# Flags of the block candidates: one comparison of all blocks on VectorE, their sum over blocks on TensorE, over tiles on ScalarE

## The chip, the cores and the metric
The kernel runs on one core of one Trainium2 chip. The metric is the device time of one execution in microseconds (us). Of the kernel before, 3 runs are given; a profile was taken in one more execution, and all durations below come from that one.

## The reference
The input is 16 batches of 512 tokens with 256 features. One transformer layer is computed, in float32: attention with 16 heads of width 16, residual and layer norm, then a gated feed-forward part (256 to 768 to 256), residual and layer norm. The attention is sparse: of the 512 scores of a row only those not below the row's 31st largest are kept.

```python
def proj(W, b):
    return (x @ W.T + b).reshape(B, L, H, D).transpose(0, 2, 1, 3)
scores = jnp.einsum('bhqd,bhkd->bhqk', Q, K) / math.sqrt(D)
top_vals, _ = jax.lax.top_k(scores, U)          # U = 31
thresh = top_vals[..., -1:]
scores = jnp.where(scores < thresh, -jnp.inf, scores)
attn = jax.nn.softmax(scores, axis=-1)
context = jnp.einsum('bhqk,bhkd->bhqd', attn, V)
...
x = _layernorm(x + attention(x))
x = _layernorm(x + (silu(x @ wg.T) * (x @ wu.T)) @ wd.T)
```

## The kernel before, in words
**Tiles and slots.** A tile is 128 query rows of one head against all 512 keys, so a batch has 16 heads x 4 = 64 tiles (`TILES`), and the kernel 1024. Every engine runs the same loop of 64 slots per batch, written out, and in slot n it works on several tiles at once, each at its own stage: the lags at the top of the file (`COUNT0 = 1`, `COUNT1 = 2`, `BELOW = 4`, ... `PV = 25`, `GROUP = 41`) say how many slots after its scores a tile comes to each stage. Semaphores tie the engines together; the order on each engine is fixed by `slots`.

**How a threshold is found.** TensorE makes a tile's scores (L593), VectorE copies them out with a shift and notes the row's maximum (`evacuate`, L859). ScalarE counts twice with Sign how many scores of a row lie above a guessed threshold (`count_first` L459, `count_second` L468); both have an accumulator output. TensorE writes the scores that lie below the guess once more into `Y_ps` (L603, L604, L606). Of each of the 4 blocks of 128 columns (`BLOCKS`) VectorE takes the 8 largest into `cand` (L866), and then the 16 largest of these 32 into `best` (L879, L882, L886). The count tells which of the 16 is the 31st of the row. That choice is made for 8 tiles (two heads) at a time, which the code calls a pair (`PAIR = 8`); there are 8 pairs in a batch and 128 in the kernel.

**The steps of a pair, on VectorE.** `pick` in slots with n % 8 = 6 marks the ranks that are not wanted (L897, 128 x 128 elements) and reduces `hidden`, the largest over the 4 blocks of each block's 8th candidate (L900). `pick_candidate` in the next slot combines the marks with `best` (L907). `pick_threshold` in slots with n % 8 = 0 reduces the chosen value (`least`, L915), compares `hidden` with it (`flag`, L917: 8 flags and, by the accumulator output, their sum as a ninth column), and adds the shift (`thr`, L921). A flag of 1 says that a block may hold more than 8 of the wanted values, so that the threshold can't be trusted.

**The way of a flag.** In the same slot TensorE adds the flags over the 128 rows, one float32 matmul against a column of ones into a PSUM bank called `bench` (`sum_flags`, L646 to L649, at the end of its slot). In the next slot ScalarE copies the 9 numbers as integers to `flag_i` (`copy_flags`, L448), behind the exponential of that slot and ahead of both counts. VectorE loads the ninth into a register after the slot's evacuation (`check`, L945); if it is above zero it loads the 8 others (L948) and finds the threshold of each flagged tile anew with four MAX8 over the whole row (`general`, L923 to L938). Then it releases the pair's thresholds to GpSimd (`thr_done`, L953), which makes the masks of its 8 tiles (`cut`, L1080, L1082 and 8 times L1088). TensorE adds the masks to the transposed scores (L617, L620), ScalarE takes the exponential (L476), TensorE multiplies by V (L634). The two `bench` banks are handed round by the semaphores `ready` and `taken`, and a flag's use of a bank is one of those of `uses_of`.

**Other work** is spread over the slots by tables: projections (L547, L578), transposes, output projection (L663), the feed-forward part (L670, L676), residuals and layer norms.

Of the kernel before, what the change touches and what calls it, by code (L numbers as in the profile page):

```python
# [12 lines left out]
P = 128  # L13
# [13 lines left out]
GONE = -3.0e38  # L27
# [13 lines left out]
BLOCKS = 4  # L41
# [21 lines left out]
RING = 32  # L63
S_PLACES = 22
MASKS = 4
CANDS = 16
PAIR = 2 * NT
# [17 lines left out]
F32 = mybir.dt.float32  # L85
F32R = mybir.dt.float32r
I32 = mybir.dt.int32
BF16 = mybir.dt.bfloat16
ALU = mybir.AluOpType
ACT = mybir.ActivationFunctionType  # L90
AX = mybir.AxisListType
# [68 lines left out]
def tile_place(part):  # L160
    return part % 2, part // 2


def build(nc, xT, x, wqT, wkT, wvT, woT, bq, bk, bv, bo, wgT, wuT, wdT, ident_in, blocks_in, heads_in, ranks_in, out):
    with ExitStack() as ctx:
        def sb(name, shape, dt=F32):
            return ctx.enter_context(nc.sbuf_tensor(name, shape, dt))

        def ps(name, shape):
            return ctx.enter_context(nc.psum_tensor(name, shape, F32))  # L170

        def sem(name):
            return ctx.enter_context(nc.semaphore(name))
# [7 lines left out]
        heads_r = sb("heads_r", [P, HALF], F32R)  # L181
        ranks = sb("ranks", [P, RANKS])
        ones = sb("ones", [1, P])
        onesc = sb("onesc", [P, 1])
        wqk = [sb(f"w{n}", [P, C, DM]) for n in "qk"]
        bqk = [sb(f"b{n}", [P, 2]) for n in "qk"]
        wv = sb("wv", [P, C, DM])
# [59 lines left out]
        cand = sb("cand", [P, CANDS, BLOCKS, 8])  # L247
# [2 lines left out]
        other = sb("other", [P, PAIR, RANKS])  # L250
        picked = sb("picked", [P, PAIR, RANKS])
        least = sb("least", [P, PAIR])
        hidden = sb("hidden", [P, PAIR])
        flag = sb("flag", [P, 2, PAIR + 1])
        flag_i = sb("flag_i", [1, 2, 16], I32)
        W = sb("W", [P, L])
        gtop = sb("gtop", [P, 4, 8])
# [7 lines left out]
        bench = [ps(f"bench{i}", [P, L]) for i in range(2)]  # L265
# [10 lines left out]
        taken = [sem(f"taken{i}") for i in range(2)]  # L276
# [14 lines left out]
        flag_done = sem("flag_done")  # L291
# [28 lines left out]
        def of_pair(a, g):  # L320

            h = 2 * g % HALF
            return a[:, 2 * g // HALF, :].rearrange("p (t h) -> p h t", h=HALF)[:, h:h + 2, :]

        def by_head(a):
            return a.rearrange("p (h t) -> p h t", h=2)
# [72 lines left out]
        def _(act):  # L399
# [42 lines left out]
            def copy_flags(b, n, first, at):  # L442
                k, use = at
                g = (n - CHECK) // PAIR
                act.wait_ge(ready[k], use + 1)
                if not (first and n < CHECK + 2 * PAIR):
                    act.wait_ge(thr_done, b * NP + g - 1)
                nc.scalar.activation(flag_i[0:1, g % 2, 0:PAIR + 1], bench[k][0:1, 0:PAIR + 1], ACT.Copy).then_inc(taken[k], 1)  # L448

            def count_first(T, n, b, first):  # L450
                j = (n - COUNT0) % TILES
# [92 lines left out]
        def _(pe):  # L544
            def project(what, hb, k):
                for c in range(C):
                    mm = nc.tensor.matmul(bench[k][:, :], wqk[what][:, c, hb * P:(hb + 1) * P], xTs[:, c, :],  # L547
                                          start=(c == 0), stop=(c == C - 1))
                return mm

            def keys(k):
                for t in range(NT):
                    mm = nc.tensor.matmul(bench[k][:, t * P:(t + 1) * P], hi[1][:, t * P:(t + 1) * P], ident_r[:, :],
                                          start=True, stop=True)
                return mm

            def gram_matrix(k):
                for t in range(NT):
                    mm = nc.tensor.matmul(bench[k][:, 0:P], Kn[:, t, :], Kn[:, t, :], start=(t == 0), stop=(t == NT - 1))
                return mm  # L560

            def quadratic(k):
                return nc.tensor.matmul(bench[k][:, :], gram[:, :], hi[0][:, :], start=True, stop=True)
# [82 lines left out]
            def sum_flags(b, n, k):  # L646
                g = (n - THRESHOLD) // PAIR
                pe.wait_ge(flag_done, b * NP + g + 1)
                return nc.tensor.matmul(bench[k][0:1, 0:PAIR + 1], onesc[:, :], flag[:, g % 2, :], start=True, stop=True)  # L649

            def turn_rows(src, k):

# [100 lines left out]
            for i, what in enumerate(PROLOGUE):  # L753
                k, use = tile_place(i)
                if use:
                    pe.wait_ge(taken[k], use)
                if what in ("q", "k"):
                    mm = project("qk".index(what), 0, k)
                if what == "keys":
                    pe.wait_ge(hi_done, 2)  # L760
                    mm = keys(k)
                if what == "gram":
                    pe.wait_ge(taken[0], 2)
                    mm = gram_matrix(k)
                if what == "quad":
                    pe.wait_ge(taken[1], 2)
                    mm = quadratic(k)
                if what == "sums":
                    pe.wait_ge(taken[0], 3)
                    mm = row_sums(k)  # L770
# [4 lines left out]
            for c in range(C):  # L775
                nc.tensor.matmul(bench[0][0:1, 0:DM], bvc[:, c:c + 1], wo[:, c, :], start=(c == 0), stop=False)
            nc.tensor.matmul(bench[0][0:1, 0:DM], ones[:, 0:1], brow[:, :],
                             start=False, stop=True).then_inc(brow_done, 1)
# [8 lines left out]
        def _(dve):  # L787
            steps = [0]

            def mark(ins):  # L790
                ins.then_inc(dve_step, 1)
                steps[0] += 1
                return steps[0]
# [94 lines left out]
            picks = {}  # L888

            def pick(b, n):  # L890

                g = (n - PICK) // PAIR
                r, e = g * PAIR % RING, g * PAIR % CANDS
                dve.wait_ge(cnt1_done, b * TILES + (g + 1) * PAIR)
                if sorted_to[0]:
                    dve.wait_ge(dve_step, sorted_to[0])
                picks["other"] = mark(nc.vector.tensor_tensor(  # L897
                    other[:, :, :], ranks[:, :].unsqueeze(1).to_broadcast([P, PAIR, RANKS]),
                    s1[:, r:r + PAIR].unsqueeze(2).to_broadcast([P, PAIR, RANKS]), ALU.not_equal))
                picks["hidden"] = mark(nc.vector.tensor_reduce(hidden[:, :], cand[:, e:e + PAIR, :, 7], AX.X, ALU.max))  # L900

            def pick_candidate(n):
                g = (n - PICKED) // PAIR
# [5 lines left out]

            def pick_threshold(n):  # L910
                g = (n - THRESHOLD) // PAIR % NP
                r, c = g * PAIR % RING, g % 2
                if "picked" in picks:
                    dve.wait_ge(dve_step, picks["picked"])
                t = mark(nc.vector.tensor_reduce(least[:, :], picked[:, :, :], AX.X, ALU.max))  # L915
                dve.wait_ge(dve_step, t)
                nc.vector.scalar_tensor_tensor(out=flag[:, c, 0:PAIR], in0=hidden[:, :], scalar=GONE, in1=least[:, :],  # L917
                                               op0=ALU.max, op1=ALU.is_gt,
                                               accum_out=flag[:, c, PAIR:PAIR + 1]).then_inc(flag_done, 1)

                picks["kept"] = mark(nc.vector.tensor_tensor(by_head(thr[:, r:r + PAIR]), by_head(least[:, :]), of_pair(na, g), ALU.add))  # L921

# [17 lines left out]
            def check(n, at):  # L940
                k, use = at
                g = (n - CHECK) // PAIR
                c = g % 2
                wait_apart(dve, taken[k], use + 1)
                some = dve.value_load(flag_i[0:1, c, PAIR:PAIR + 1], min_val=0, max_val=PAIR * P)  # L945
                with dve.If(some > 0):
                    for t in range(PAIR):
                        flagged = dve.value_load(flag_i[0:1, c, t:t + 1], min_val=0, max_val=P)  # L948
                        with dve.If(flagged > 0):
                            general((g * PAIR + t) % TILES)  # L950
                if "kept" in picks:
                    dve.wait_ge(dve_step, picks["kept"])
                dve.nop(nofuse=True).then_inc(thr_done, 1)  # L953
# [225 lines left out]
```

## Time and profile before

| | |
|---|---|
| median of 3 runs | 3387.09 us |
| lowest, highest | 3374.43, 3392.51 us |
| the profiled execution, its own time | 3384.81 us |
| its span | 3383.0 us |
| mean granted TensorE clock | 0.913 of full speed |
| busy share: TensorE / VectorE / ScalarE / GpSimd | 83% / 76% / 71% / 71% |

The span runs from the first to the last instruction; 1.8 us of the execution lie outside it. PE is TensorE's matmuls, PEld its weight loads, DVE VectorE, ACT ScalarE, POOL GpSimd, and a trailing q an engine's sequencer, which handles waits, registers and branches. An instruction with an accumulator output shows as two, the second of which is named READ_ACCUMULATOR.

### The profile page before, as it was taken

To read this page: it belongs to the slowest core of one execution; us is meant where nothing else is said; L and a number is where in the kernel's file an instruction comes from. 1 tells how busy PE (TensorE), PEld (TensorE's weight loads), DVE (VectorE), ACT (ScalarE), POOL (GpSimd) and SP (SyncE) were. 2 spreads that over 40 slices of the span, in tenths; PEclk is the share of its full clock that TensorE was granted. 3 is DMA by queue.
4 is the path that set the end of the run, shared out by engine and by line. 5 is a ranking of instruction groups with operands and counts; after the bars stand their busy time and mean duration, and the time that the engine had idled before them with its cause. 6 is when DMAs were issued, how large, how long until landed. Compare 5 with 4: busy or idle time off the path is not lost.

```text
span 3383.0 us, 82396 instructions
## 1 busy us (share of the span) xinstructions
PE 2808.2 (83%) x21094; PEld 1534.9 (45%) x21439; DVE 2587.7 (76%) x12511; ACT 2414.3 (71%) x5894; POOL 2405.8 (71%) x1677
## 2 busy tenths in 40 slices
PE   5889899697989888776998999987789976886986
PEld 2344545344444444433544454544445443443454
DVE  4888788787878787777887888887778877777861
ACT  4788787686868787665786788886668865675862
POOL 2787788586777786656786787876668865675881
PEclk7799999899999898987998999998889988898986
DMA  3101011110101111011110111111011110111000
GB/s 82 43 23 43 22 41 31 33 26 19 44 24 35 25 35 35 18 32 23 27 42 21 36 24 46 27 37 32 17 33 27 46 25 15 33 26 27 20 14 7
DMA packets 91071, 102.84 MB, mean 30 GB/s; under 512 B 34417, under 2 KB 52850, under 8 KB 90482
## 3 DMA queue, kind: packets, MB, share of 16 engines
q1 hardware_dynamic: 88448, 93.73, 11.6%
q8 instruction: 186, 3.05, 0.4%
q14 instruction: 403, 3.30, 0.3%
q10 hardware_dynamic: 2034, 2.76, 0.2%
HBM read 20.86 MB, written 8.39 MB: 9 GB/s over the span
## 4 chain that ended last, share of the span: by engine, by line
PE 44%; DVE 19%; issue 15%; ACT 11%; POOL 4%; DVEq 4%; SPq 1%; ACTq 0%; DMA 0%; POOLq 0%
DVE cand L866 6%; PE Y_ps L606 5%; PE bench L676 5%; PE ST_ps L620 5%; PE ST_ps L617 5%; PE ctxT_ps L634 5%; PE bench L670 4%; ACT junk L459 4%; PE Y_ps L604 3%; POOL mask L1088 3%; ACT above L468 3%; DVEq L948 3%; PE bench L547 2%; ACT PT L476 2%; DVE S L859 2%
## 5 line engine op out<-in xcount | busy, mean ns | idle before, releaser
L1088 POOL TENSOR_SCALAR mask<-S,thr,mb 128x512 bf16<-128x512 f32 x1024 | 2117.6, 2084 | 43.0 <-POOL mb L1082 24.8
L866 DVE MAX8 cand<-Y_ps 128x8 f32<-128x128 f32 x4096 | 1069.2, 281 | 9.9 <-issue 9.8
L459 ACT ACTIVATE junk<-S,nt 128x512 bf16<-128x512 f32 x1024 | 733.7, 716 | 476.4 <-DVE S L859 472.9
L859 DVE TENSOR_SCALAR_CACHE_REDUCE S<-S_ps,na 128x512 f32<-128x512 f32 x1024 | 755.6, 738 | 298.8 <-PE S_ps L593 246.4
L468 ACT ACTIVATE above<-S,s,steep 128x512 bf16<-128x512 f32 x1024 | 822.5, 803 | 0.0
L476 ACT ACTIVATE PT<-ST_ps 128x512 f32<-128x512 f32 x1024 | 596.6, 583 | 199.0 <-PE ST_ps L620 196.6
L1080 POOL TENSOR_SCALAR rbig<-rmax 128x8 f32<-128x8 f32 x128 | 31.3, 244 | 755.2 <-DVEq L953 755.1
L617 PE MATMUL ST_ps<-QS,KS 64*128 64x512 f32 x1024 | 463.4, 453 | 94.3 <-ACT PT L476 89.7
L593 PE MATMUL S_ps<-KS,QS 64*128 64x512 f32 x1024 | 532.3, 520 | 4.2 <-DVE S L859 2.2
L606 PE MATMUL Y_ps<-KS,QS 64*128 64x512 f32 x1024 | 532.1, 520 | 1.0 <-issue 0.7
L604 PE MATMUL Y_ps<-above,nbig 128*128 128x512 bf16 x1020 | 406.6, 399 | 146.8 <-DVE cand L866 107.6
L603 PE MATMUL Y_ps<-ones_b,nbig 128*128 128x512 bf16 x683 | 276.6, 405 | 268.7 <-DVE cand L866 259.7
L620 PE MATMUL ST_ps<-nbig,mask 128*128 128x128 bf16 x4096 | 424.3, 229 | 0.0
L606 PEld LDWEIGHTS Y_ps<-KS,QS 64*128 64x128 f32 x1024 | 195.1, 190 | 469.0 <-issue 469.0
L620 PEld LDWEIGHTS ST_ps<-nbig,mask 128*128 128x128 bf16 x4096 | 241.4, 100 | 339.7 <-issue 339.7
L634 PE MATMUL ctxT_ps<-PT,V 128*32 128x128 f32 x8192 | 346.6, 289 | 0.0
L603 PEld LDWEIGHTS Y_ps<-ones_b,nbig 128*128 128x128 bf16 x1024 | 101.4, 99 | 502.2 <-issue 450.4
L879 DVE MAX8 best<-cand 128x8 f32<-128x32 f32 x1024 | 191.9, 187 | 142.9 <-issue 140.9
L617 PEld LDWEIGHTS ST_ps<-QS,KS 64*128 64x128 f32 x1024 | 199.9, 195 | 203.2 <-ACT PT L476 195.4
L634 PEld LDWEIGHTS ctxT_ps<-PT,V 128*32 128x32 f32 x8192 | 201.2, 113 | 57.9 <-issue 7.2
L593 PEld LDWEIGHTS S_ps<-KS,QS 64*128 64x128 f32 x1024 | 195.3, 191 | 5.3 <-DVE S L859 3.3
L459 ACT ACTIVATION_READ_ACCUMULATOR junk<-S,nt 128x1 f32 x1024 | 196.3, 192 | 0.0
(121 smaller groups left out, 3837.7 us busy)
## 6 DMA issues: line engine op xcount, KB each, us to landing
QS<-Qhi SPq DMA_DIRECT2D x512, 32.0 KB, 2.0
KS<-Khi SPq DMA_DIRECT2D x512, 32.0 KB, 2.0
KS<-Klo SPq DMA_DIRECT2D x512, 32.0 KB, 2.0
QS<-Qlo SPq DMA_DIRECT2D x512, 32.0 KB, 2.0
xTs<-in_xT SPq DMA_DIRECT2D x17, 512.0 KB, 3.8
xs<-in_x SPq DMA_DIRECT2D x16, 512.0 KB, 3.9
out<-xs SPq DMA_DIRECT2D x16, 512.0 KB, 2.9
hT<-in_wgT ACTq DMA_DIRECT2D x1, 768.0 KB
```

The costliest lines, as they stand in the source:

```text
L459: nc.scalar.activation(junk[:, :], S[:, score_place(j)[0], :], ACT.Sign, bias=nt0[:, hb, col:col + 1], scale=-1.0, accum_out=s0[:, j % 8:j ...
L468: nc.scalar.activation(above[:, j % 4, :], S[:, score_place(j)[0], :], ACT.Sign, bias=s0[:, j % 8:j % 8 + 1], scale=steep[:, hb, col:col + ...
L476: nc.scalar.activation(PT[:, j % 4, :], ST_ps[:, :], ACT.Exp, scale=SCALE).then_inc(exp_done, 1)
L593: nc.tensor.matmul(S_ps[n % 2][:, :], QS[rows, r, q:q + P], KS[rows, r, :], start=True, stop=True, tile_position=(rows.start, 0)).then_inc ...
L604: nc.tensor.matmul(Y[:, :], nbig[:, :], above[:, j % 4, :], start=False, stop=False)
L606: nc.tensor.matmul(Y[:, :], QS[rows, r, q:q + P], KS[rows, r, :], start=False, stop=True, tile_position=(rows.start, 0)).then_inc(below_do ...
L617: nc.tensor.matmul(ST_ps[:, :], KS[rows, r, kt * P:(kt + 1) * P], QS[rows, r, :], start=True, stop=False, tile_position=(rows.start, 0))
L620: mm = nc.tensor.matmul(ST_ps[:, t * P:(t + 1) * P], mask[:, h % MASKS, t, kt * P:(kt + 1) * P], nbig[:, :], start=False, stop=(t == NT - 1))
L634: mm = nc.tensor.matmul(ctxT_ps[32 * a:32 * a + 32, strip * P:(strip + 1) * P], V[:, k, grp, strip * VW:strip * VW + 32], PT[:, (j - kt + ...
L859: nc.vector.tensor_scalar(S[:, at, :], S_ps[n % 2][:, :], na[:, hb, col:col + 1], None, ALU.add, op1=ALU.max, accum_out=rmax[:, n % RING:n ...
L866: mx = nc.vector.max(cand[:, j % CANDS, i, :], Y_ps[j % 2][:, i * BW:(i + 1) * BW])
L1088: nc.gpsimd.tensor_scalar(mask[:, h % MASKS, t, :], S[:, score_place(j)[0], :], thr[:, r:r + 1], mb[:, r:r + 1], ALU.is_lt, op1=ALU.add).t ...
```

## The change
VectorE no longer reduces `hidden`. Instead it compares all 4 blocks' 8th candidates with `least` in one tensor_tensor, whose 128 x 32 flags are written as bfloat16. TensorE adds the blocks by 4 accumulating bfloat16 matmuls of 8 columns (one per block, each reading every fourth flag). ScalarE's copy now covers 8 columns and makes their sum by its accumulator output, in float32; VectorE reads its bits as an integer, which is above zero where the sum is.

```diff
-        onesc = sb("onesc", [P, 1])
+        onesc = sb("onesc", [P, 1], BF16)
...
-        hidden = sb("hidden", [P, PAIR])
-        flag = sb("flag", [P, 2, PAIR + 1])
+        flag = sb("flag", [P, 2, PAIR, BLOCKS], BF16)
...
-                nc.scalar.activation(flag_i[0:1, g % 2, 0:PAIR + 1], bench[k][0:1, 0:PAIR + 1], ACT.Copy).then_inc(taken[k], 1)
+                nc.scalar.activation(flag_i[0:1, g % 2, 0:PAIR], bench[k][0:1, 0:PAIR], ACT.Copy,
+                                     accum_out=flag_i[0:1, g % 2, PAIR:PAIR + 1].bitcast(F32)).then_inc(taken[k], 1)
...
-                return nc.tensor.matmul(bench[k][0:1, 0:PAIR + 1], onesc[:, :], flag[:, g % 2, :], start=True, stop=True)
+                for i in range(BLOCKS):
+                    mm = nc.tensor.matmul(bench[k][0:1, 0:PAIR], onesc[:, :], flag[:, g % 2, :, i], start=(i == 0),
+                                          stop=(i == BLOCKS - 1))
+                return mm
...
-                picks["hidden"] = mark(nc.vector.tensor_reduce(hidden[:, :], cand[:, e:e + PAIR, :, 7], AX.X, ALU.max))
...
-                nc.vector.scalar_tensor_tensor(out=flag[:, c, 0:PAIR], in0=hidden[:, :], scalar=GONE, in1=least[:, :],
-                                               op0=ALU.max, op1=ALU.is_gt,
-                                               accum_out=flag[:, c, PAIR:PAIR + 1]).then_inc(flag_done, 1)
+                nc.vector.tensor_tensor(flag[:, c, :, :], cand[:, e:e + PAIR, :, 7],
+                                        least[:, :].unsqueeze(2).to_broadcast([P, PAIR, BLOCKS]),
+                                        ALU.is_gt).then_inc(flag_done, 1)
...
-                some = dve.value_load(flag_i[0:1, c, PAIR:PAIR + 1], min_val=0, max_val=PAIR * P)
+                some = dve.value_load(flag_i[0:1, c, PAIR:PAIR + 1], min_val=0, max_val=0x45000000)
...
-                        flagged = dve.value_load(flag_i[0:1, c, t:t + 1], min_val=0, max_val=P)
+                        flagged = dve.value_load(flag_i[0:1, c, t:t + 1], min_val=0, max_val=BLOCKS * P)
```

## Rows read from the trace of the kernel before

**Rows 1.** The page: busy time by engine, the chain that ended last.
```profile
PE 2808.2 (83%) x21094; PEld 1534.9 (45%) x21439; DVE 2587.7 (76%) x12511; ACT 2414.3 (71%) x5894; POOL 2405.8 (71%) x1677
...
PE 44%; DVE 19%; issue 15%; ACT 11%; POOL 4%; DVEq 4%; SPq 1%; ACTq 0%; DMA 0%; POOLq 0%
```

**Rows 2.** The chain in order of time, 1055.9 to 1060 us: start, us, what.
```profile
1056.16 0.42 PE Y_ps L606
...
1056.65 0.76 DVE S L859 x2
1057.41 0.21 DVE least L915
...
1058.15 0.08 DVE flag L917
...
1059.82 0.38 PE Y_ps L604
```

**Rows 3.** Timeline of VectorE around a pick: start, us, engine, line, operation, shapes.
```profile
1033.05 0.20 DVE L900 TENSOR_REDUCE hidden<-cand 128x8 f32<-128x32 f32 x1
1033.17 0.18 DVE L879 MAX8 best<-cand 128x8 f32<-128x32 f32 x1
```

**Rows 4.** The chain's pieces at L900: the first and the last of 33.
```profile
70.72 0.12 DVE hidden L900
...
3107.41 0.13 DVE hidden L900
```

**Rows 5.** Single lines of VectorE: duration in ns, minimum/median/maximum.
```profile
L897 DVE TENSOR_TENSOR other<-ranks,s x128: 278/286/1554, 70.4 to 3272.9; 128x128 f32<-128x128 f32 x128
...
L917 DVE SCALAR_TENSOR_TENSOR flag<-hidden,least x128: 166/170/1402, 75.1 to 3274.4; 128x8 f32<-128x8 f32 x128
...
L921 DVE TENSOR_TENSOR thr<-least,na x128: 159/166/1380, 75.2 to 3274.5; 128x8 f32<-128x8 f32 x128
```

**Rows 6.** Groups of VectorE by line: busy us, mean ns of one, idle before.
```profile
L917 DVE SCALAR_TENSOR_TENSOR flag<-hidden,least 128x8 f32<-128x8 f32 x128 | 45.3, 354 | 4.4
...
L900 DVE TENSOR_REDUCE hidden<-cand 128x8 f32<-128x32 f32 x128 | 26.2, 205 | 0.0
...
L917 DVE DVE_READ_ACCUMULATOR flag<-hidden,least 128x1 f32 x128 | 10.2, 80 | 0.0
```

**Rows 7.** Timeline around a stretched comparison: VectorE, then GpSimd.
```profile
1143.86 0.67 DVE L917 SCALAR_TENSOR_TENSOR flag<-hidden,least 128x8 f32<-128x8 f32 x1
...
1144.46 0.08 DVE L917 DVE_READ_ACCUMULATOR flag<-hidden,least 128x1 f32 x1
1144.46 0.16 DVE L921 TENSOR_TENSOR thr<-least,na 128x8 f32<-128x8 f32 x1
...
1143.75 2.07 POOL L1088 TENSOR_SCALAR mask<-S,thr,mb 128x512 bf16<-128x512 f32 x1
```

**Rows 8.** Timeline of TensorE around the sum of flags; then its matmuls alone.
```profile
1146.48 0.14 PEld L649 LDWEIGHTS bench<-flag,onesc 128*1 128x1 f32 x2
...
1146.54 0.20 PE L649 MATMUL bench<-flag,onesc 128*1 128x9 f32 x2
...
L649 PE MATMUL bench<-flag,onesc x256: 170/173/222, 76.6 to 3281.4; 128*1 128x9 f32 x128
```

**Rows 9.** The chain at matmuls of 8 columns with 128 columns of weights.
```profile
1169.65 0.11 PE bench L569
```

**Rows 10.** The chain's pieces at L649: the first and the last of 37.
```profile
96.95 0.13 PE bench L649 x2
...
3238.26 0.03 PE bench L649
```

**Rows 11.** Timeline of ScalarE around the copy of flags.
```profile
1147.22 0.15 ACT L448 ACTIVATE flag_i<-bench 1x9 int32<-1x9 f32 x1
...
1147.28 0.71 ACT L459 ACTIVATE junk<-S,nt 128x512 bf16<-128x512 f32 x1
...
1147.89 0.18 ACT L459 ACTIVATION_READ_ACCUMULATOR junk<-S,nt 128x1 f32 x1
...
1147.99 0.80 ACT L468 ACTIVATE above<-S,s,steep 128x512 bf16<-128x512 f32 x1
```

**Rows 12.** The chain's pieces at L448: the first and the last of 13.
```profile
340.75 0.15 ACT flag_i L448
...
3216.31 0.02 ACT flag_i L448
```

**Rows 13.** A check that waits for its flags: the copy, the load, VectorE's next work.
```profile
L448 ACT ACTIVATE flag_i<-bench x1: 153/153/153, 1220.9 to 1220.9; 1x9 int32<-1x9 f32 x1
...
L945 DVEq TENSOR_LOAD <-flag_i x1: 307/307/307, 1221.3 to 1221.3; - x1
...
1222.61 0.20 DVE L879 MAX8 best<-cand 128x8 f32<-128x32 f32 x1 [0.68 <-issue]
```

**Rows 14.** A check that doesn't: the same three.
```profile
L448 ACT ACTIVATE flag_i<-bench x1: 153/153/153, 1060.3 to 1060.3; 1x9 int32<-1x9 f32 x1
...
L945 DVEq TENSOR_LOAD <-flag_i x1: 304/304/304, 1061.0 to 1061.0; - x1
...
1062.35 0.19 DVE L879 MAX8 best<-cand 128x8 f32<-128x32 f32 x1 [0.43 <-issue]
```

**Rows 15.** The chain in an opened pair, and the count of tile loads.
```profile
1121.34 0.30 DVEq L948
...
1122.16 0.31 DVEq L948
...
L948 DVEq TENSOR_LOAD <-flag_i x184: 298/303/910, 119.6 to 3127.4; - x184
```

**Rows 16.** Waits, the longest in total: us, times, longest.
```profile
POOL rbig L1080 <- DVEq L953: 755.1, 107, 37.0
```

More of the change, by code:

```diff
@@ L892, in pick @@
                 g = (n - PICK) // PAIR
-                r, e = g * PAIR % RING, g * PAIR % CANDS
+                r = g * PAIR % RING
                 dve.wait_ge(cnt1_done, b * TILES + (g + 1) * PAIR)
@@ L911, in pick_threshold @@
                 g = (n - THRESHOLD) // PAIR % NP
-                r, c = g * PAIR % RING, g % 2
+                r, c, e = g * PAIR % RING, g % 2, g * PAIR % CANDS
                 if "picked" in picks:
```

## The prediction
> **What bounds the kernel now.** I read the shares of the engines first, then the chain of work that ended last. No engine is full: TensorE 83% busy, VectorE 76%, ScalarE and GpSimd 71% [rows 1]. The chain stands on TensorE for 44%, on VectorE for 19%, on ScalarE for 11%, on GpSimd for 4% [rows 1], and changes engine within a few microseconds: at 1056 us it leaves TensorE for VectorE's evacuation, passes through the very instructions of the change, and is back on TensorE at 1059.8 [rows 2]. So no engine's busy time can be used as a price. The change takes a little from VectorE and puts a little on TensorE and ScalarE, once in each of 128 pairs. I therefore price each edit by the time that its engine is held until it starts the next instruction, and multiply by the pairs in which the chain stands on that engine there. All sums start from the profiled execution, 3384.81 us, 2.3 us below the median of the runs.
>
> **The reduction of `hidden` goes.** It lasts 205 ns [rows 6], but the next MAX8 starts 0.12 us after it [rows 3], and the chain gives it 0.12 us too [rows 4]. The chain holds it in 33 of 128 pairs [rows 4]: 33 x 0.12 = -4.0 us. Elsewhere VectorE reaches its next wait earlier; that is worth nothing while TensorE or ScalarE sets the pace. Bounds: 0, and 128 x 0.12 = -15.4 us if VectorE paced every pair.
>
> **The comparison changes form.** The row before is a comparison of 8 elements, median 170 ns. The new one has 32 elements and no accumulator. A tensor_tensor of 8 elements takes 166 ns, one of 128 elements 286 ns [rows 5], 1.0 ns an element, so 32 make about 190 ns: 0.02 us more. The accumulator's read of 80 ns [rows 6] starts in the same instant as the next instruction at 1144.46 [rows 7], so I credit nothing for it. I find the chain on VectorE at the comparison in 48 pairs: 48 x 0.02 = +1.0 us. The bounds are -0.08 us a pair, if the read does hold the engine, and +0.02 us.
>
> The mean of the old comparison is 354 ns against the median of 170 [rows 5, 6]: 128 x 0.184 = 23.6 us of stretch. In the row shown it lasts 0.67 us, while GpSimd's mask has started 0.11 us before [rows 7]. Both the old and the new form read two tensors of SBUF, so the stretch should stay, and I cost it at 0. If it went, 48 of 128 pairs' share would be -8.9 us; if timing moved more comparisons into a mask's start, as much could be added.
>
> **TensorE.** Before, one float32 matmul runs as two weight loads and two passes; both together last 0.20 us, one alone 0.17 [rows 8], so a further pass costs 0.03 us. The change makes four weight loads and four bfloat16 passes: two more, +0.06 us. The bound above is the 0.11 us of a pass of 8 columns that loads 128 weight columns [rows 9], +0.22 us; below, nothing. I take 0.06, since its row has one weight column as the new ones have. The chain holds L649 in 37 pairs [rows 10], and stands on TensorE there in 41: 41 x 0.06 = +2.5 us (0 to 9; over all pairs 7.7).
>
> The Trainium skill, "TensorE: Matmul & The Clock Gate", section "Back-to-back issue gap", speaks against this: streams of weight load and matmul are spaced by about 81 ns at 128 columns, whereas an isolated matmul of 1 to 64 columns has a floor near 25 ns. By the first, two more would cost 0.16 us, as an estimate, and this term would be 6.6 us; the row of two passes 0.03 us apart is on the side of the second.
>
> **ScalarE.** The copy holds the engine for 0.06 us (1147.22 to 1147.28). An accumulator output adds a read; behind that of the first count the next instruction starts 0.10 us after the read [rows 11], 0.09 us in most places. So +0.09 us a pair: the exponential of the slot is ahead of it, both counts behind it and with them TensorE's L604 and the next exponential. The chain stands on ScalarE at the copy in 21 pairs, in 13 of which it holds the copy itself [rows 12]: 21 x 0.09 = +1.9 us (bounds 0 and 128 x 0.09 = 11.5).
>
> **The flag comes later to the check.** The copy signals after 0.15 us now; with the read it is 0.06 + 0.19 = 0.25 us [rows 11], and where ScalarE waited for TensorE, 0.06 more: 0.15 us late. Queued behind the check on VectorE are the sort of the next tile and its evacuation; GpSimd waits for it 755 us in all [rows 16]. A load that waits for the copy starts some 0.17 us after the copy's end. There are 9 such pairs among 128, the one at 1220.9 shown; VectorE then sits idle for 0.68 us [rows 13] instead of 0.43 [rows 14]. All others have more time: the next 24 loads start 0.34 to 0.42 us after the copy's end, 0.17 us or more to spare. So 9 x 0.15 = +1.4 us.
>
> **What stays.** The flagged tiles are the same: the largest of four values exceeds `least` exactly when one of them does. 184 tile loads are 23 opened pairs [rows 15], after as before. DMAs and the other uses of the banks are untouched.
>
> **The sum.** -4.0 + 1.0 + 2.5 + 1.9 + 1.4 = +2.8 us; 3384.8 + 2.8 = 3387.6, and I give 3388. A measurement of this kernel can tell about 0.5% from no change, 17 us.
>
> **Rival 1, VectorE paces more than the chain shows: faster.** Then each pair gives back its 0.12 us (-15.4), the comparison is no longer held by GpSimd on the chain (-8.9), and ScalarE's +1.9 remains: 3384.8 - 22.4 = 3362. For it: the chain's 15% of issue time, much of it VectorE's sequencer. Against it: the wait of ScalarE and GpSimd is mostly for other things than these instructions, and the new form has two SBUF inputs as well. The Trainium skill, "SBUF — State Buffer", section "SBUF: two separate sides", says that a VectorE operation with two SBUF inputs and a GpSimd operation exclude each other for a whole instruction; the trace shows the exclusion, but its comparison ended 0.78 us into a mask of 2.07 us. By that rule too the new form is held as the old. Chance 0.12.
>
> **Rival 2, the late flag becomes a new wait: slower.** Place: the load of the check. If the flag is late by d, 9 pairs pay d, 24 pay d less about 0.2, and 20 more, whose load starts 0.42 to 0.6 us after the copy, pay d less about 0.34. At d = 0.6 us, from four weight loads that wait for one another and an accumulator that drains slowly, this is 5.4 + 9.6 + 5.2 = 20 us, and 3405 in all. It decides from d of about 0.55 us; I expect 0.15. Chance 0.10.
>
> **Rival 3, the change doesn't do what it says: slower.** If the bits of the float sum, or the integer conversion, opened pairs without a flag, each would cost 8 loads 0.8 us apart [rows 15], 6.4 us; 105 unflagged pairs make at most 670 us, and 20 already 128: 3513. The sum of zeros has zero bits, so I give 0.02.
>
> **How the numbers follow.** My case has 0.76. Its own range: the gains at their bound and the losses at none give 3384.8 - 15.4 = 3369; TensorE's at 9, ScalarE's at 11.5 and the check's 1.4 with no gain give 3407. The runs shown themselves spread over 18 us. Leaving the corners out, 3371 to 3406 should hold 8 in 10; Rival 1's point and Rival 3 lie outside, Rival 2's just inside. Faster by over 0.5%: Rival 1's 0.12, of which some falls short of 17 us, and scatter of the runs in my case: 0.12. Slower: Rivals 2 and 3 with scatter, 0.13. Within: 0.75.
>
> **What would show it.** In the changed profile: no L900 group, VectorE busy down by some 26 + 10 us less 3 for the longer comparison; the comparison's median near 190 ns with maxima above 1 us still; TensorE's group of the flags with 512 short passes, first to last within 0.3 us; a READ_ACCUMULATOR of 0.19 us behind the copy, ScalarE busy up by some 25 us; 184 tile loads. Wrong would be: a chain that gives the check or the flags' matmuls 20 us more, a comparison never above 0.2 us, more than 184 tile loads, or another granted clock than 0.91.

## The result, and the profile after

The changed kernel takes 3410.53 us (median of 8 runs, 3401.91 to 3418.27), the kernel before 3385.31 us beside it (8 runs, 3374.43 to 3398.04): a ratio of 1.0078, with a 95% interval of 1.006 to 1.0095. That is 25 us slower, 22 us above the forecast of 3388 and above the upper end of its range, 3406.

The page of the changed kernel, busy time by engine, the chain's shares and the queue of instruction transfers:

```profile
span 3406.6 us, 83125 instructions
...
PE 2885.9 (85%) x21695; PEld 1551.2 (46%) x21695; DVE 2579.7 (76%) x12255; ACT 2429.4 (71%) x6022; POOL 2404.5 (71%) x1677
...
q14 instruction: 400, 3.28, 0.3%
...
PE 45%; DVE 20%; issue 15%; ACT 11%; DVEq 4%; POOL 3%; SPq 1%; ACTq 0%; DMA 0%; POOLq 0%
```

Beside [rows 1] this hardly shows a change. VectorE has 8 us less work, ScalarE 15 us more; the records of TensorE can't be compared this closely, since [rows 1] hold 21094 matmuls beside 21439 weight loads, where each matmul has one. No engine took over the chain.

The groups that the change touches, by line (busy us, mean ns of one, idle before):

```profile
L921 DVE TENSOR_TENSOR flag<-cand,least 128x32 bf16<-128x32 f32 x128 | 48.7, 380 | 4.4
...
L448 ACT ACTIVATION_READ_ACCUMULATOR flag_i<-bench 1x1 f32 x128 | 23.8, 186 | 0.0
...
L448 ACT ACTIVATE flag_i<-bench 1x8 int32<-1x8 f32 x128 | 19.8, 155 | 3.2 <-PE bench L651 1.1
```

And the same as single lines, with minimum, median and maximum in ns:

```profile
L651 PE MATMUL bench<-flag,onesc x512: 167/168/214, 76.2 to 3306.7; 128*1 128x8 bf16 x171
...
L921 DVE TENSOR_TENSOR flag<-cand,least x128: 207/219/1424, 74.7 to 3298.9; 128x32 bf16<-128x32 f32 x128
...
L952 DVEq TENSOR_LOAD <-flag_i x184: 296/303/890, 120.0 to 3146.4; - x184
```

The reader is to see that every instruction of the change is of the kind and nearly of the length that was forecast, and that there are still 184 tile loads, 23 opened pairs [rows 15]. A pair's flags in the timeline of 1060 to 1075 us, for the four passes and the late sum:

```profile
1068.26 0.24 PEld L651 LDWEIGHTS bench<-flag,onesc 128*1 128x1 bf16 x4
1068.37 0.25 PE L651 MATMUL bench<-flag,onesc 128*1 128x8 bf16 x4
...
1069.59 0.15 ACT L448 ACTIVATE flag_i<-bench 1x8 int32<-1x8 f32 x1
1069.65 0.19 ACT L448 ACTIVATION_READ_ACCUMULATOR flag_i<-bench 1x1 f32 x1
```

Where the time went shows only in the waits. Waits of the changed kernel (idle us, times, the longest one):

```profile
POOL rbig L1084 <- DVEq L957: 776.6, 113, 35.9
...
DVE best L883 <- issue: 159.6, 112, 6.4
```

Of the kernel before, the same view has for the second line:

```profile
DVE best L879 <- issue: 140.9, 114, 6.4
```

GpSimd waits 21.5 us longer for the release of the pairs' thresholds (755.1 [rows 16]; L957 is the release that was L953), and VectorE stands 18.7 us longer before the sort L883 that follows the check, for "issue", which is nothing that the profile shows. The release is a step that the change doesn't touch.

### The profile page after: what moved, and what is told of

The parts are those of the page before. It is cut to its first block, busy times and chain, and to the rows that moved or that the text cites. A ratio compares the mean times of both kernels' runs of the same rounds, so it can differ in the third digit from the quotient of the medians.

```text
span 3406.6 us, 83125 instructions
## 1 busy us (share of the span) xinstructions
PE 2885.9 (85%) x21695; PEld 1551.2 (46%) x21695; DVE 2579.7 (76%) x12255; ACT 2429.4 (71%) x6022; POOL 2404.5 (71%) x1677
## 3 DMA queue, kind: packets, MB, share of 16 engines
q14 instruction: 400, 3.28, 0.3%
## 4 chain that ended last, share of the span: by engine, by line
PE 45%; DVE 20%; issue 15%; ACT 11%; DVEq 4%; POOL 3%; SPq 1%; ACTq 0%; DMA 0%; POOLq 0%
DVE cand L870 7%; PE Y_ps L607 5%; PE bench L680 5%; PE bench L674 5%; PE ST_ps L618 5%; PE ST_ps L621 5%; PE ctxT_ps L635 4%; ACT junk L460 4%; PE Y_ps L604 3%; PE Y_ps L605 3%; PE bench L548 3%; DVEq L952 3%; ACT above L469 3%; DVE S L863 3%; POOL mask L1092 2%
## 5 line engine op out<-in xcount | busy, mean ns | idle before, releaser
L870 DVE MAX8 cand<-Y_ps 128x8 f32<-128x128 f32 x4096 | 1081.1, 286 | 7.3 <-issue 7.0
L604 PE MATMUL Y_ps<-ones_b,nbig 128*128 128x512 bf16 x1024 | 414.0, 404 | 364.9 <-DVE cand L870 351.3
L883 DVE MAX8 best<-cand 128x8 f32<-128x32 f32 x1024 | 195.0, 190 | 161.6 <-issue 159.6
```

The lines of the kernel that those rows point to most:

```text
L604: nc.tensor.matmul(Y[:, :], nbig[:, :], ones_b[:, :], start=True, stop=False)
L870: mx = nc.vector.max(cand[:, j % CANDS, i, :], Y_ps[j % 2][:, i * BW:(i + 1) * BW])
```

## The parts by themselves

The first four kernels ran on one chip. `a_full` is the changed kernel again, and the reference for the three others.

> The whole change again, on the chip of the three below, so that the parts are compared with it and with the kernel before on one chip. Every theory: 3410 us, ratio 1.0078 or so, granted clock near 0.906.

Measured: 3402.7 us, ratio 1.0039 (1.0022 to 1.0056), span 3407.5 us. The same code was timed twice more (below), with 1.0077 and 1.0078. So four timings of one kernel gave 1.0039 to 1.0078, and differences of 0.4% between two kernels of this study are to be read with care.

**TensorE alone**: the flags and the column of ones in bfloat16, and the same nine columns added four times.

```diff
-                return nc.tensor.matmul(bench[k][0:1, 0:PAIR + 1], onesc[:, :], flag[:, g % 2, :], start=True, stop=True)
+                for i in range(BLOCKS):
+                    mm = nc.tensor.matmul(bench[k][0:1, 0:PAIR + 1], onesc[:, :], flag[:, g % 2, :],
+                                          start=(i == 0), stop=(i == BLOCKS - 1))
+                return mm
```

> TensorE's part alone: the flags and the ones are bfloat16, and the same nine columns are added four times. Theory 1 (the parts add up by their occupancy): four passes cost 0.06 us more in 41 pairs, +2.5 us, 3388. Theory 2 (TensorE's part carries the change, since the flags' passes stand on TensorE's own path): +15 to 20 us, 3402. Theory 3 (small shifts move the clock's dips and code fetches): anywhere between 3380 and 3405, with the granted clock going along.

Measured: 3379.66 us, 0.9983 (0.9968 to 0.9998), span 3382.5. Two more passes a pair cost nothing that is seen.

**ScalarE alone**: the copy of 8 columns with the accumulator output, everything else as before.

> ScalarE's part alone: 8 columns are copied and their sum is made by the accumulator output. Theory 1: +0.09 us in 21 pairs and a check later by 0.10 us in 9, +3 us, 3388. Theory 4 (ScalarE holds the path longer than the chain showed, up to all 128 pairs): +0.1 x 128 = +13 us, 3398. If it is above 3398, the late flag of Rival 2 is in play and the idle of VectorE behind the check grows.

Measured: 3386.46 us, 0.9999 (0.9986 to 1.0013), span 3385.7. The read is there, at 185 ns, and the flag comes as late to the check as in the change. It costs nothing:

```profile
L448 ACT ACTIVATION_READ_ACCUMULATOR flag_i<-bench 1x1 f32 x128 | 23.7, 185 | 0.0
```

**The change without ScalarE's part**: VectorE writes the sum itself, as a ninth row, and ScalarE copies 9 columns.

```diff
-                nc.vector.tensor_tensor(flag[:, c, :, :], cand[:, e:e + PAIR, :, 7],
-                                        least[:, :].unsqueeze(2).to_broadcast([P, PAIR, BLOCKS]),
-                                        ALU.is_gt).then_inc(flag_done, 1)
+                nc.vector.scalar_tensor_tensor(out=flag[:, c, 0:PAIR, :], in0=cand[:, e:e + PAIR, :, 7], scalar=GONE,
+                                               in1=least[:, :].unsqueeze(2).to_broadcast([P, PAIR, BLOCKS]),
+                                               op0=ALU.max, op1=ALU.is_gt,
+                                               accum_out=flag[:, c, PAIR, 0:1]).then_inc(flag_done, 1)
```

> The change with ScalarE's part undone: the comparison of 32 elements sums its own flags by an accumulator output, TensorE adds four passes of nine columns, ScalarE copies nine. Theory 1: 3410 less 3 = 3407. Theory 4: 3410 less 13 = 3397. Theory 2 (TensorE's part carries the change): 3408. If VectorE's new comparison is what costs, 3408 or above.

Measured: 3396.8 us, 1.0034 (1.0021 to 1.0048), span 3393.9. So the loss comes with VectorE's part: the parts that leave VectorE's instructions alone lose nothing, and the two kernels in which a pair has fewer of them lose. Their own durations don't explain it: the new comparison is 0.05 us longer (219 ns against 170), which makes 6 us in all 128 pairs, and what was taken out should gain, not lose.

## A check that stalls

The page doesn't show what differs at the check, single instances do. The same check (batch 5, slot 25) is quick in the kernel before: load at 1061.0 [rows 14], and the release 1.2 us later:

```profile
L953 DVEq EVENT_SEMAPHORE  x1: 21/21/21, 1062.2 to 1062.2; - x1
```

In `a_full` (line, duration, first to last start; the second line is the release):

```profile
L949 DVEq TENSOR_LOAD <-flag_i x1: 305/305/305, 1067.6 to 1067.6; - x1
...
L957 DVEq EVENT_SEMAPHORE  x1: 21/21/21, 1071.2 to 1071.2; - x1
```

VectorE's timeline around it, and GpSimd's:

```profile
1067.80 0.73 DVE L863 TENSOR_SCALAR_CACHE_REDUCE S<-S_ps,na 128x512 f32<-128x512 f32 x1
1068.46 0.08 DVE L863 DVE_READ_ACCUMULATOR S<-S_ps,na 128x1 f32 x1
1071.38 0.20 DVE L883 MAX8 best<-cand 128x8 f32<-128x32 f32 x1 [2.83 <-issue]
...
1065.49 2.07 POOL L1092 TENSOR_SCALAR mask<-S,thr,mb 128x512 bf16<-128x512 f32 x1
1071.35 0.24 POOL L1084 TENSOR_SCALAR rbig<-rmax 128x8 f32<-128x8 f32 x1 [3.79 <-DVEq L957]
```

The release comes 3.55 us after the load, VectorE is idle for 2.83 us instead of 0.43 [rows 14], and GpSimd with it. The flag was zero: no tile load lies between. VectorE's sequencer only had to branch over the block that finds flagged tiles anew. The kernel before has the same stall in other places, such as batch 2, slot 9, which is quick in `a_full` (1.18 us):

```profile
L945 DVEq TENSOR_LOAD <-flag_i x1: 303/303/303, 416.3 to 416.3; - x1
...
L953 DVEq EVENT_SEMAPHORE  x1: 21/21/21, 420.0 to 420.0; - x1
```

```profile
416.87 0.08 DVE L859 DVE_READ_ACCUMULATOR S<-S_ps,na 128x1 f32 x1
420.16 0.20 DVE L879 MAX8 best<-cand 128x8 f32<-128x32 f32 x1 [3.21 <-issue]
```

Of the 128 checks, 105 open no pair in every kernel. From load to release they take 1.18 us (median); a few take 2.2 to 3.8. Taken over all 105, from the trace of each:

| | sum, us | over 1.5 us |
|---|---|---|
| before | 148.2 | 12 |
| TensorE alone, ScalarE alone | 147.9, 147.5 | 12, 12 |
| changed kernel, and `a_full` | 155.0, 155.2 | 16, 16 |
| change without ScalarE's part | 161.1 | 21 |

The stalls belong to places in the code, not to moments: VectorE's loop holds five batches written out, and a stalled check stalls again five batches later (in `a_full` slot 25 of batches 5, 10 and 15, slot 57 of batches 3, 8 and 13). Before, TensorE alone and ScalarE alone have one and the same set. The change takes two instructions a pair out of VectorE's code, L900 and the accumulator's read behind L917, so that each later check sits at another place.

Counted in instructions along VectorE's stream (the skipped block is 136 of them), the checks of the kernel before, of `a_full` and of the change without ScalarE's part that take over 2.1 us are those at which the jump lands on number 62 to 78 of a run of 128. Every closed check that lands on 62 to 77 stalls; of two places that land on 78 one does; none that lands elsewhere takes more than 1.7 us. The count can be off by one or two. 128 instructions are, if the 8192 bytes of one instruction transfer (400 transfers with 3.28 MB on the page above) are theirs, 64 bytes each. The trace's records of these transfers agree: after a quick check's load one of 8192 bytes starts at about 1.78 us, 0.6 us behind the release; after that of 763.26 us in `a_full` one starts at 1.64 us, a second at 4.17, and the release, at 3.56, lies behind the first. This holds beyond the two. In the kernel before, each of the 12 stalled checks has one transfer of 8192 bytes that starts between its load and its release, and the release comes 1.76 to 2.01 us behind that start; in the 93 other closed checks none starts there. (In `a_full` 3 of 89 quick checks have one as well, 0.2 to 0.4 us behind the load.) That is how I read it: the engine waits for code.

The Trainium skill, "Runtime: NRT & Kernel Launch", section "Instruction fetch mechanics", says that code is fetched ahead in sequence and that a "taken branch whose target isn't in the current 2-page window forces a DMA fetch of the target page before execution can continue". The traces agree with that, and show its price here, 1.1 to 2.5 us a branch. That section of the Trainium skill gives blocks of 16 KiB or 256 instructions; here VectorE's stalls repeat with 128, and the transfers beside them have 8192 bytes.

## Moving the code and nothing else

If place is the cause, a kernel with other places and the same work must show it. The first try put instructions of the sequencer alone, `dve.nop(nofuse=True)`, ahead of VectorE's loop.

> The whole change, with 26 empty instructions ahead of VectorE's first wait for loads, so that all its later code lies 26 instructions further on and nothing else differs. In the traces so far a closed check (one that opens no pair) takes 1.18 us from its load to its release, or 2.2 to 3.7 us, and the slow ones come back every 5 batches, which is the unrolling of VectorE's loop. Theory L (the place of the branch's target in VectorE's code decides: slow where it falls on instruction 62 to 78 of every 128, counted from the trace's first): slow closed checks cost 6 us instead of 28 to 31, 3402.7 - 22 = 3380, granted clock up to 0.915. Theory T (it is timing, not place): 3403, with the same 16 slow checks.

> The whole change, with 39 empty instructions at the same place. Theory L: 23 checks' places are slow, 48 us in all, 20 more than unshifted: 3403 + 20 = 3423. Theory T: 3403.

> The kernel before, with 111 empty instructions at the same place. Theory L: slow checks cost 5 us instead of 25, 3387 - 20 = 3367. Theory T: 3387. Against the change shifted by 26, which has about the same cost of slow checks, it gives the change without its effect on the code's place: under the predicted sum of parts 3 us apart; if more than 10 us apart, the new comparison or the way of the flags costs by itself.

> The kernel before, with 78 empty instructions at the same place. Theory L: slow checks cost 41 us instead of 25, 3387 + 16 = 3403, as slow as the change. Theory T: 3387.

Measured: 1.0077 (1.0057 to 1.0096), 1.0078 (1.0059 to 1.0098), 0.9999 (0.9984 to 1.0013), 0.9998 (0.9984 to 1.0013). The stalled checks are the same ones as without the instructions, 16 and 12 of them: a nop that signals nothing left nothing in the code, and these four are repeats of the two kernels. What they say is how well a repeat agrees: within 0.1% on one chip.

The second try used memsets of one column of a tensor that nothing reads, once, ahead of VectorE's first wait:

```diff
+        filler = sb("filler", [P, P])
...
+            for _ in range(78):
+                nc.vector.memset(filler[:, _:_ + 1], 1.0)
```

> As b_full26, but with 26 real instructions: memsets of one column of an unused tensor ahead of VectorE's first wait for loads, where it idles for 11 us. (The trace of b_full26 shows that the empty instructions had not been kept: VectorE's code began as before and the same 16 closed checks were slow, so those four runs were repeats of the change and of the kernel before.) Theory L (place in VectorE's code): slow closed checks at 6 us over the usual 1.18 each instead of 31: 3410 - 25 = 3385 or, where TensorE's clock gains too, 3378. Theory T (timing, not place): 3410, 16 slow checks.

> The change with 39 such memsets. Theory L: some 23 slow closed checks, 48 us in all, 17 to 20 more than unshifted: 3410 + 18 = 3428. Theory T: 3410.

> The kernel before with 111 such memsets. Theory L: slow checks 5 us in all instead of 25: 3385 - 20 = 3365. Theory T: 3385. The change shifted by 26 against this one is the change without the code's place.

> The kernel before with 78 such memsets. Theory L: slow checks 41 us in all instead of 25: 3385 + 16 = 3401. Theory T: 3385.

| | ratio | interval | sum of the 105 checks, us | over 1.5 us |
|---|---|---|---|---|
| change + 26 | 1.0053 | 1.0035 to 1.0071 | 132.9 | 8 |
| change + 39 | 1.0072 | 1.0056 to 1.0089 | 175.5 | 26 |
| before + 111 | 0.9982 | 0.9971 to 0.9993 | 145.3 | 15 |
| before + 78 | 1.0111 | 1.0091 to 1.0132 | 170.0 | 25 |

The last row shows that place alone can cost this much. It is the kernel before, without any part of the change, its code 78 instructions further on, and it takes 3422.05 us, 37 us more than the kernel before on the same chip (3385.08) and more than the change. Its span, and the waits of GpSimd for the release:

```profile
die 0 (median of its cores): 3423.2 us, clock 0.908
```

```profile
POOL rbig L1083 <- DVEq L954: 795.0, 112, 35.5
```

40 us of wait more than in [rows 16], 21.8 us of it in the closed checks themselves. One of them, batch 5, slot 57, takes 1.16 us before and 3.63 here:

```profile
1189.23 0.08 DVE L860 DVE_READ_ACCUMULATOR S<-S_ps,na 128x1 f32 x1
1192.53 0.19 DVE L880 MAX8 best<-cand 128x8 f32<-128x32 f32 x1 [3.22 <-issue]
```

The unused tensor and the memsets themselves are not the cause: before + 111 has the same tensor and more memsets, and is 0.2% faster than the kernel before.

Only the direction of the last two rows came as expected, and no size did. Before + 111 is 9 us faster where 20 were expected, before + 78 37 us slower where 16 were. Change + 39, expected 18 us above the change, has 20 us more in its checks and is not slower than the change (1.0072 against 1.0068, the mean of its timings). The first row is a plain miss: with the fewest stalled checks of all it is still 0.5% slower. And change + 26 against before + 111, named ahead as the change without its effect on place, with 3 us between them if the sum of the parts holds and over 10 us if the new instructions cost by themselves, came out 25 us apart (3401.44 and 3376.33). So the sum of the checks is not the whole effect of place, and this pair alone would speak for a cost of the change's own.

## The change with its code back in place

If the change loses by place and its own instructions cost what the prediction said, then the change with VectorE's code of the old length must land at the sum of the prediction, +2.8 us. `d_restored` is the change with one memset of one column where L900 was and one behind the new comparison, so that every check, and every jump, sits where it sat before.

```diff
                 picks["other"] = mark(nc.vector.tensor_tensor(
...
+                nc.vector.memset(filler[:, 0:1], 0.0)
...
                                         ALU.is_gt).then_inc(flag_done, 1)
+                nc.vector.memset(filler[:, 1:2], 0.0)
```

> The whole change, with two real instructions per pair put where it took two out of VectorE's code: a memset of one unused column behind the marks of the pick, one behind the new comparison. All of VectorE's later code lies where it lay before the change. Each memset may hold VectorE 0.02 to 0.06 us, so its 0.12 us of gain is mostly kept. Theory L (the lost time is the place of the code): 12 slow closed checks, 1.4 us or less a batch over before, 3385 + 0 to 5 = 3388. Theory C (the new comparison and the later flags cost by themselves): 3400 or more, with 12 slow checks all the same.

Measured: 3389.69 us beside 3384.81, ratio 1.0011 (1.0 to 1.0022), span 3395.0. It has exactly the stalled checks of the kernel before, 12 with a sum of 147.6 us. The check of batch 5, slot 25, is quick again:

```profile
L952 DVEq TENSOR_LOAD <-flag_i x1: 303/303/303, 1061.7 to 1061.7; - x1
...
L960 DVEq EVENT_SEMAPHORE  x1: 21/21/21, 1062.9 to 1062.9; - x1
```

```profile
1062.56 0.09 DVE L864 DVE_READ_ACCUMULATOR S<-S_ps,na 128x1 f32 x1
1063.06 0.20 DVE L884 MAX8 best<-cand 128x8 f32<-128x32 f32 x1 [0.42 <-issue]
```

So the change with 256 instructions more is 0.3 to 0.7% faster than the change in its four timings (1.0039 to 1.0078) and within 5 us of the kernel before. Two memsets were added to each pair and nothing of the change was taken out, so in this layout the change's own instructions cost 0 to 7 us. That the memsets help in another way than by place was not tested.

**Trying to remove the stalls** from all kernels was less clear. Memsets inside the block that a closed check skips make the jump longer, so each landing place can be chosen, for a code place of its own at each check, and only an opened pair's eighth tile, if flagged, would run them. `d_before_clear` and `d_change_clear` test whether the branch's own place decides: by their filling no branch of a later check starts in the stretch from which it would reach 62 to 78 over a block of 136, wherever it lands.

```diff
                         with dve.If(flagged > 0):
                             general((g * PAIR + t) % TILES)
+                            if t == PAIR - 1:
+                                for i in range(next(skipped)):
+                                    nc.vector.memset(filler[:, i:i + 1], 0.0)
```

> The kernel before, with memsets of an unused tensor put inside the block that a closed check jumps over (0 to 36 behind the eighth tile's search), so chosen that no later check's branch lies in the bad window. They are executed only where the eighth tile of a pair is flagged, 3 or so times. Theory L, and the branch's own place decides: at most one closed check over 1.5 us, closed checks 124 us in all instead of 148, 3385 - 24 or, at the slope that 78 memsets showed (1.6 us per us), -38: 3347 to 3361. If the target's place decides, slow checks move to others and the time stays within 10 us of 3385.

> The same for the changed kernel: no slow closed check. Theory L: as d_before_clear within 5 us (the parts' sum says +3). Theory C: 15 us or more above d_before_clear.

Measured: 1.0043 (1.0027 to 1.0059) with 19 stalled checks, 1.0022 (1.0009 to 1.0035) with 14. The stalled ones are all among the checks with 22 to 41 memsets in their block, and land on 69 to 88. So the branch's own place doesn't decide it; some of these landings lie in 62 to 78, as the count by landing says, and some behind it, where the three kernels above had no such stall. The next three used at most 17 memsets a check and a rule of both, the place of the branch and that of its landing.

> The kernel before with the filling chosen anew. d_before_clear had 19 slow closed checks, each with its jump's target at 69 to 88 of the 128, and no slow one with the branch alone inside the window: so a jump is slow where it starts before instruction 78 of 128 (in the target's count, 137 further on) and lands behind 61. Now at most 13 instructions are put into any skipped block, so that no closed check of the loop does that. Theory L: no closed check over 2 us, 124 to 128 us in all instead of 148; the time falls by 20 to 35 us: 3350 to 3365. If the time does not fall by 10 us, the waits at the checks are not what the place of the code costs.

> The same for the changed kernel: no closed check over 2 us. Theory L: within 6 us of e_before_clear (the parts' sum says 3 above). Theory C (the comparison and the flags' way cost by themselves): 15 us or more above it.

> a_pe (only TensorE's four bfloat16 passes, 0.17% below before) with the filling of e_before_clear; its VectorE code is that of before. A candidate to beat both kernels: 5 us below e_before_clear if the gain of a_pe is real, the same if it was scatter.

Measured: 0.9989 (0.9974 to 1.0004) with 18 stalls, 1.0041 (1.0027 to 1.0056) with 13, and 1.0 (0.9982 to 1.0018) with 16 for the TensorE part with the fillings of the first. The rule failed again, and none of the three beats the kernel before. In `e_before_clear` the check of slot 17 in batches 5 and 10, which has no filling, lands on about 81 and takes 3.6 and 3.8 us; in the change without ScalarE's part a check that lands there takes 1.2. So 62 to 78 isn't the whole rule for a block of 136 either, and the exact law of the stall stays open.

Both pairs of fillings were also to tell a cost of the change's own from place; its sign was to be the changed kernel 15 us or more above the other. The first pair has the changed kernel 7 us below the other (3391.3 and 3398.47), the second 17 us above it (3401.07 and 3383.72), with 13 stalls against 18. By that measure the second is on the side of an own cost and the first is not.

## What the clock has in it

Each run comes with its span and mean granted clock. The 129 executions of the kernel before that ran beside the experiments have a median span of 3383.5 us at a clock of 0.914, and among them 0.01 less clock goes with 17 us more span. That is scatter of one and the same code. Brought to 0.910 by that slope:

| | executions | median span, us | median clock | at 0.910, us |
|---|---|---|---|---|
| before | 129 | 3383.5 | 0.914 | 3390 |
| change, all four timings | 32 | 3406.5 | 0.907 | 3402 |
| change, places restored | 12 | 3387.9 | 0.913 | 3394 |
| before + 78 | 4 | 3420.2 | 0.908 | 3414 |
| change + 26 | 6 | 3399.6 | 0.914 | 3406 |

Of the change's 23 us, some 12 are there at an equal clock, and 11 go along with a mean clock lower by 0.007. The closed checks, 7 us longer in all, may make 7 of the 12. On top come stalls a few instructions behind a release (2.0 us between a MAX8 and a MATCH_VALUE_LOAD in `a_full`, batch 2, slot 17); that these add up to the rest was not worked out. Whether stalls lower the clock, by leaving TensorE idle, or whether it is a lower clock in other ways, no run separates. With the places restored the clock is back at 0.913, and 4 us are left at an equal clock.

## Why the prediction was wrong

**The step that failed** is "What stays". It listed the flagged tiles, the tile loads, the DMAs and the banks, and left out the place of VectorE's code. The change part "The reduction of `hidden` goes" priced the instruction's time, and no term priced that two instructions fewer a pair shift every later branch against the blocks in which code arrives. That term is about +20 us here (1.0078 less the restored change's 1.0011, of 3385 us, is 22.7 us; by the mean of the change's four timings, 1.0068, it is 19, by the lowest of them 9), larger than the sum of all others and of either sign: 0.9982 to 1.0111 for the kernel before alone. The trace of before had its sign of it: 12 checks of 105 with 2.3 to 3.7 us, where the row of a check not waiting [rows 14] has 1.2, and the group of L879 with 140.9 us of "issue". The working took a check that waits for ScalarE and one that waits for nothing as samples, and the one of [rows 14] as the like of all others.

**The sum of the parts held**, as far as one layout can tell. It gave +2.8 us; the restored change measured +4.9 by the medians and +3.7 by the ratio (0 to 7). By term:

- L900, -4.0: not seen as a gain in the end. From one evacuation to the next, summed over the kernel, the interval with the pick got shorter by 11.0 us in `a_full` (12.3 in `d_restored`), and the following one longer by 13.4 (8.3). What VectorE gains there it gives back within a slot. The upper bound of 15.4 was the right size for the gain, and 0 for the outcome.
- The comparison, +0.02 us a pair: mis-sized. The median is 219 ns, not 190, and the next instruction starts 0.128 us after it against 0.093 before. At 48 pairs this makes +1.7 to +2.4 us instead of +1.0.
- The stretch by GpSimd, 0: right. The mean is 380 ns above a median of 219, 128 x 0.161 = 20.6 us, beside 23.6; the maximum is 1.42 us.
- TensorE, +0.06 us a pair: right in size. Four passes last 0.25 us where two lasted 0.20 [rows 8], so they are 0.03 us apart or less, and the 81 ns a pass of the Trainium skill, "TensorE: Matmul & The Clock Gate", section "Back-to-back issue gap", were not met here. On the path: not the +2.5 us but nothing (0.9983).
- ScalarE, +0.09 us a pair: right in size, 0.06 and then 0.09 us to the next instruction. On the path it cost nothing that is seen (0.9999).
- The late flag, +1.4: within what ScalarE's part alone shows, nothing.

**The rivals.** Rival 1 (faster) is false: with the places restored nothing is gained, and the stretch stays. Rival 2 gave nearly the right time, 3405 us, by luck, since its mechanism is not what happened: GpSimd does wait longer for the release, but `a_act` and `d_restored` have the same late flag and lose 0 and 0.1%. Rival 3 is false: 184 tile loads, and the 23 opened checks take some 310 us in all in every kernel.

**The signs.** None of those that were to show it wrong came in the form given. The chain doesn't give the check 20 us more: VectorE's sequencer has 4% of it and issue time 15%, as before, and the 20 us are seen only in the waits, where they look like Rival 2. The comparison's median is 219 ns and not near 190. VectorE is busy 8 us less where 33 less were expected: the comparison and L900 went nearly as forecast, but other instructions, the MAX8 of the blocks above all with 1081.1 us against 1069.2, were busy longer in this execution; in `a_full` that MAX8 has 1068.8 us.

The chance of 0.13 for slower was too low for a further reason: the range was built from the terms alone, and a kernel with 128 such branches has a spread from its layout, here of about 1.3% between the extremes of one program (0.9982 and 1.0111), that any edit of VectorE's code draws from anew.

**Still open:** the exact law of the stall; why the change + 26, with the fewest stalled checks, is still 0.5% slower; how the clock and the stalls hang together; and whether the change has a cost of its own beside its place. With the places restored it is 0.2% at most; but its six layouts gave 1.0011 to 1.0078 and the five of the kernel before 0.9982 to 1.0111, and of the three pairs that were to tell, two point to such a cost.

## What to carry to other kernels

Where an engine branches over a block of many instructions in each turn, read its checks one by one: load to release, and the idle time put down to "issue" behind it. If a few places take two to three times as long, and again after each turn of the unrolled loop, look whether a transfer of code starts beside each of them. Here it did, and adding or removing an instruction on that engine dealt the slow places out anew. Before a difference below 1% is believed of such a kernel, time it at two or three layouts, with cheap instructions that keep or move the code: a change that loses 0.8% may be worth nothing either way once its branches are put back.

## What was not expected of the hardware

- A branch on VectorE over 136 instructions takes 1.18 us from the load of its register to the release behind it, but 2.2 to 3.8 us at some places, which repeat with 128 instructions; 78 instructions ahead of everything made one and the same program 1.1% slower.
- An added pass of TensorE with one weight column and 8 bfloat16 columns, and a read of 186 ns on ScalarE, cost nothing that was seen, 128 times each (0.9983 and 0.9999).
- Within one program the time followed the mean granted clock: 17 us of 3385 for 0.01.
